# Gated cross-attention and mixture of experts on one core: ten instead of twelve row-maximum tiles ahead of the attention, the turn of the maxima one step later, and rows of ones spread by transfers

## The chip, the core and the metric

The kernel runs on one core of one Trainium2 chip. A core has five engines that run their own instruction lists side by side: PE (TensorE, matrix products, with PEld for its weight loads), DVE (VectorE), ACT (ScalarE), POOL (GpSimd) and SP (SyncE, which here only issues DMA transfers). They wait for each other through semaphores. The metric is the device time of one launch in microseconds. The kernel before took 764.62 us in the median of 3 runs (763.82 to 765.73).

## What is computed

The reference, cut to what matters (4 batches, 512 queries, 1024 keys, width 256, 16 heads of width 16, 8 routed experts of which each token takes 2, and one shared expert):

```python
q, k, v = heads(layernorm(x) @ Wq.T + bq), heads(ctx @ Wk.T + bk), heads(ctx @ Wv.T + bv)
attn = softmax(q @ k.T / 4) @ v
x = x + tanh(g_xattn) * (join_heads(attn) @ Wo.T + bo)
h = layernorm(x)
cw = top2(softmax(h @ gate_w + gate_b))
x = x + tanh(g_ffn) * (swiglu_expert(h, shared) + sum_e cw[e] * swiglu_expert(h, e))
```

The biases and weights are scaled so that products of plain bfloat16 numbers would be too coarse. So queries and keys are split into three bfloat16 parts each, and six products of parts are stacked as 96 rows of the contraction.

## The kernel before

**Phase A** (PE lines up to L1396) makes queries, keys and values, batch by batch. For each batch PE multiplies three 512-wide blocks: two of the context (keys and values) and one of the normalised x (queries). ACT copies and adds the bias (`biased`, L744 and L745, and the value copies L753), DVE makes the second parts (L1002, L1003), the rounding remainders (L979) and the layer norm (`variances`, L951 to L957, and `normalise`, L962 to L968), POOL makes the third parts (L575). SP stores all of it to DRAM and loads it back in the stacked layout as `qst` and `kst`. `kst` holds the keys of four slots; slot u is heads 4u to 4u+3. Rows 96 to 98 of `kst` are ones; the same rows of `qst` are filled with the three bfloat16 parts of the negated row maximum of the scores. A score matmul contracts all 99 rows, so the maximum is subtracted inside the product.

At its very start POOL sets those three rows of ones for all slots with one memset (L554), after two memsets on `vst`. DVE then works out the layer norm of the first batch, ACT takes a square root in it (L716), and PE turns the normalised rows (`turn`, L1324) between its first and its second block.

**The attention** is 16 units (4 batches by 4 slots), each of 8 steps (one per 128 keys). What PE does in step k of a unit is written out by hand: the scores of heads 0 and 1 for the step two ahead (`LEAD = 2`, L1423), the products with the values for this step (L1450), the scores of heads 2 and 3 for two steps ahead, and then two maximum tiles (`max_tile`, L1405). A maximum tile is the 128 by 1024 score block of one head and 128 queries; DVE reduces it to 128 negated maxima (L1058). ACT takes the exponentials of the scores (L795).

Each unit needs 16 such tiles. They run ahead: `FIRST` = 12 of the next unit's are made before the attention begins, for unit 1. Then the steps of unit n make the 4 that are missing for unit n+1 (steps 0 and 1) and 12 for unit n+2 (steps 2 to 7). When unit n+1 has its 16, its maxima go this way:

1. PE turns them with a 128 by 16 transpose at the end of step `MAX_TURN` = 2 (`turn_max`, L1334).
2. ACT copies the result in step `MAX_COPY` = 3, behind the exponentials of its first head (`copy_max`, L772).
3. POOL splits it into three bfloat16 parts with four small instructions (`split_max`, L561 to L567).
4. SP sends each part into a row of `qst` (`load_max`, three transfers, L400).
5. PE waits for the three transfers (`m_ld`) before the first score of unit n+1. That score is made two steps ahead, so it stands at the start of step 6 of unit n. All that PE has after it in its list waits too.

Between phase A and the loop PE runs the `FIRST` maximum tiles and, from the sixth on, one of the first 8 scores beside each (`BEFORE = 5`). In unit 0 POOL has one more instruction ahead of its first split in the loop: it multiplies the output bias by the gate (L614), and waits for that bias, which SP loads at L454 behind the loads of slots 2 and 3.

**The end of the attention.** In the last units no later unit is left to make maxima for. Unit 14 makes only the missing ones for unit 15. After those the router and output projection begin beside the attention, from step 3 of unit 14 (`ROUTER_AT`, stages 0 to 12): PE turns stored attention outputs (`r_attn`, L1511) and multiplies them with the output weights (L1518). Stage 0 waits until all maxima are reduced, since it writes where they were. From `TAIL` on, the scores of heads 2 and 3 also go into room of the maxima. On SP, the transfers of unit 15's maxima are queued behind two loads (L473) that wait for the router's turns of stages 0 and 2.

**After it** come the shared expert, the routing table, and 39 tiles of 128 routed tokens through their experts (L1656 to L1694), added to the output by POOL.

Of the kernel before, what the change touches and what calls it, by code (L numbers as in the profile page):

```python
# [29 lines left out]
BF16 = mybir.dt.bfloat16  # L30
# [6 lines left out]
P = 128  # L37
# [3 lines left out]
QT = NQ // P  # L41
KT = NK // P
HG = 4
NG = NH // HG
UNITS = NB * NG
TERMS = ((0, 0), (0, 1), (1, 0), (1, 1), (0, 2), (2, 0))
SROWS = len(TERMS) * DH
MROWS = SROWS + 3
# [17 lines left out]
BLK = 512  # L66
# [4 lines left out]
def build(nc, x, ctx_in, gates, wqkv, bqkv, wo, bo, gate_w, gate_b, wexp, b1, b2, ident, tri, out):  # L71
# [11 lines left out]
    with ExitStack() as es:  # L83
        sb = lambda name, shape, dt=F32, st=es: st.enter_context(nc.sbuf_tensor(name, shape, dt))
        ps = lambda name, shape, st=es: st.enter_context(nc.psum_tensor(name, shape, F32))
        sem = lambda name: es.enter_context(nc.semaphore(name))
# [9 lines left out]
        W0 = nc.sbuf_base  # L96
# [4 lines left out]
        b1_p = sb("b1_p", [NE * 4, 3, P], BF16, sP)  # L101
        sP.close()
        sb("early_weights", [P, EARLY, WU, UNIT], F32R)
        trimask = sb("trimask", [P, NR, NR])
        tg_in = sb("tg_in", [P, 2])
        tg = sb("tg", [P, 2])
# [65 lines left out]
        kst = sb("kst", [MROWS, NG, HG, NK], BF16, sB)  # L172
# [53 lines left out]
        v_full = sem("v_full"); v_taken = sem("v_taken")  # L226
        qk_st = [sem(f"parts_stored{c}") for c in range(3)]
        v_st = [sem(f"v_stored{s}") for s in range(4)]
        pads = sem("pads"); ones_k = sem("ones_k"); cw_ones = sem("cw_ones")
        unit_ld = [sem(f"unit_in{s}") for s in range(NG)]  # L230
        m_ld = [sem(f"max_in{s}") for s in range(NG)]
        m_full = sem("m_full"); m_free = sem("m_free")
# [60 lines left out]


        TILES = HG * QT
        FIRST = 12
        REST = TILES - FIRST
        AHEAD = TILES + FIRST
        MAX_TURN = 2
        MAX_COPY = 3  # L300
        LEAD = 2


# [8 lines left out]

        TAIL = KT * (UNITS - 2) + 2 + LEAD
        ROUTER_AT = KT * (NG - 2) + 3

        def score_bank(s, j):
# [10 lines left out]
        def max_tiles(u, step):  # L329

            for j in (2 * step, 2 * step + 1):
                yield (j, 1, FIRST + j) if j < REST else (j, 2, j - REST)

        def exists(last, u):
            return not last or u < NG
# [5 lines left out]
        def _(sp):  # L341
# [41 lines left out]
            def load_unit(b, u):  # L383

                for t, (qp, kp) in enumerate(TERMS):
                    rows = slice(t * DH, (t + 1) * DH)
                    heads = slice(u * HG * DH, (u + 1) * HG * DH)
                    sp.dma_start(qst[rows, u], q_parts[b, qp, heads, :].rearrange("(h d) t -> d h t", d=DH)
                                 ).then_inc(unit_ld[u], 16)
                    sp.dma_start(kst[rows, u], k_parts[b, kp, heads, :].rearrange("(h d) t -> d h t", d=DH)  # L390
                                 ).then_inc(unit_ld[u], 16)
# [10 lines left out]
            def first_unit():  # L402

                for c in range(3):
                    sp.wait_ge(qk_st[c], 32 + 32)
                load_unit(0, 0)

            stores(0, True)
            stores(1, True, first_unit)
# [125 lines left out]
        def _(pool):  # L535
# [15 lines left out]
            nc.gpsimd.memset(vst[:, :, :, :, DH:DH + 1].rearrange("p a b h v -> p (a b h) v"), 1.0).then_inc(pads, 1)  # L551
            pool.wait_ge(pads, 1)

            nc.gpsimd.memset(kst[SROWS:MROWS], 1.0).then_inc(ones_k, 1)  # L554
            pool.wait_ge(ones_k, 1)


            def split_max(n, parity):
# [153 lines left out]
        def _(act):  # L712
# [88 lines left out]
            def unit_exps(b, u, last):  # L801
                n = 4 * b + u
                for k in range(KT):
                    ahead = exists(last, u + (k + LEAD) // KT)
                    for j in range(HG):
                        if ahead:
                            exponentials(8 * n + k + LEAD, (k + LEAD) % 4, j)
                        if k == MAX_COPY and j == 0 and exists(last, u + 1):

# [126 lines left out]
        def _(dve):  # L936
# [123 lines left out]

            for i in range(FIRST):
                reduce_tile(TILES + i, 1, i)
# [250 lines left out]
        def _(pe):  # L1313
# [112 lines left out]

            pe.wait_ge(f_taken, 2 + 6 * NB)
            pe.wait_ge(v_taken, 2 + 4 * NB)
            pe.wait_ge(ones_k, 1)
            pe.wait_ge(unit_ld[1], 16 * 12)  # L1430
            BEFORE = 5
            for i in range(FIRST):
                max_tile(TILES + i, 1, i)
                if i == BEFORE:
                    pe.wait_ge(m_ld[0], 48)
                if i >= BEFORE:
                    score_tile((i - BEFORE) // HG, 0, (i - BEFORE) // HG, (i - BEFORE) % HG)
            for i in range(FIRST - BEFORE, LEAD * HG):
                score_tile(i // HG, 0, i // HG, i % HG)
# [14 lines left out]
            def unit(b, u, last):  # L1454
                n = 4 * b + u
                for k in range(KT):
# [17 lines left out]
                    for j, off, i in tiles:  # L1474
# [3 lines left out]
                        max_tile(AHEAD + TILES * n + j, (u + off) % NG, i)  # L1478
                    if k == MAX_TURN and exists(last, u + 1):
                        turn_max(n + 1, (u + 1) % 2, AHEAD + TILES * n + REST)  # L1480
# [289 lines left out]
```

## Time and profile before

| | |
|---|---|
| span of the profiled execution | 764.7 us |
| median of 3 runs (lowest, highest) | 764.62 us (763.82, 765.73) |
| PE busy | 672.2 us, 88% |
| DVE busy | 498.5 us, 65% |
| ACT busy | 425.6 us, 56% |
| POOL busy | 238.4 us, 31% |
| 240 maxima reductions on DVE, L1058 | 282.6 us, 1220 ns each |
| 488 score matmuls into psS, L1423 | 154.3 us, 389 ns each |
| 1024 value matmuls, L1450 | 138.5 us, 613 ns each |
| 480 maximum matmuls, L1405 | 128.0 us, 387 ns each |
| mean granted TensorE clock | 0.948 of full |

Busy time says how long an engine had an instruction running; matmuls overlap, so a busy PE counts each stretch once. The span is one execution by the profiler. The share of PE over the whole is a mean over stages: phase A up to 121 us, the attention up to about 541 us, the shared expert and routing up to about 607 us, and the routed tiles. What a change is worth is read in its own stage.

### The profile page before, as it was taken

Reading aid. Unit: us, or ns where it says so; the run is one execution under the profiler, and the core shown is the slowest. Engines: PE = TensorE matmul, PEld = TensorE weight load, DVE = VectorE, ACT = ScalarE, POOL = GpSimd, SP = SyncE. Lnnn points to the kernel's source line nnn. Section 1 sums busy time; section 2 is a strip of 40 time slices with the busy share of each in tenths; the row PEclk is TensorE's granted clock in tenths of the full one; section 3 lists DMA queues with packets and bytes.
Section 4 is the critical chain, followed back from the end, with each engine's and each line's share of the span. In section 5 each row is a group of like instructions: output and inputs, shape, how many; then the busy total and the mean of one; then the engine's idle time right before and its main releaser. Section 6 shows DMA issues by size and latency. Waiting matters only on the chain.

```text
span 764.7 us, 12596 instructions
## 1 busy us (share of the span) xinstructions
PE 672.2 (88%) x3616; PEld 337.7 (44%) x3616; DVE 498.5 (65%) x791; ACT 425.6 (56%) x842; POOL 238.4 (31%) x236
## 2 busy tenths in 40 slices
PE   3787659699999999999999999788669899999980
PEld 3675532133333333333333333433547677777750
DVE  5899888578888888888888886375267433232320
ACT  3665345467777777777777777455122234343430
POOL 8433232312434224430002221001744024444441
PEclk9999898899999999999999999899979999999995
DMA  8799769665677976787634500100795524545334
GB/s 268 275 241 361 138 228 167 101 97 104 177 163 145 212 185 188 163 164 140 92 57 69 101 1 2 55 0 9 269 427 189 155 51 86 86 80 86 59 45 125
DMA packets 80954, 106.36 MB, mean 139 GB/s; under 512 B 15616, under 2 KB 62890, under 8 KB 79949
## 3 DMA queue, kind: packets, MB, share of 16 engines
q1 hardware_dynamic: 70400, 78.04, 43.6%
q0 software_dynamic: 10512, 27.79, 14.0%
q8 instruction: 22, 0.36, 0.2%
q14 instruction: 20, 0.16, 0.1%
HBM read 62.10 MB, written 45.60 MB: 141 GB/s over the span
## 4 chain that ended last, share of the span: by engine, by line
PE 71%; issue 13%; DVE 5%; POOL 4%; DMA 3%; another core or an unknown queue 2%; SPq 1%; ACT 0%; POOLq 0%; DVEq 0%; ACTq 0%
PE psO L1450 16%; PE psS L1423 15%; PE psM L1405 12%; PE psH L1668 8%; PE psY L1694 4%; POOL parts L575 3%; PE psH L1624 2%; PE psH L1665 2%; PE psX L1518 1%; PE psH L1679 1%; PE psX L1656 1%; PE psY L1691 1%; PE psO L1493 1%; DMA acc<-ysb,zg 1%
## 5 line engine op out<-in xcount | busy, mean ns | idle before, releaser
L795 ACT ACTIVATE pr<-psS 128x512 f32<-128x512 f32 x488 | 266.6, 595 | 108.8 <-PE psS L1423 108.7
L1058 DVE TENSOR_REDUCE mneg<-psM 128x1 f32<-128x1024 f32 x240 | 282.6, 1220 | 68.1 <-PE psM L1405 68.0
L1423 PE MATMUL psS<-qst,kst 99*128 99x512 bf16 x488 | 154.3, 389 | 11.2 <-DMA qst<-msb 10.7
L1450 PE MATMUL psO<-pr,vt 128*32 128x512 f32 x1024 | 138.5, 613 | 0.0
L1405 PE MATMUL psM<-kst,qst 96*128 96x512 bf16 x480 | 128.0, 387 | 6.4 <-DVE mneg L1058 4.1
L1423 PEld LDWEIGHTS psS<-qst,kst 99*128 99x128 bf16 x488 | 40.0, 97 | 160.0 <-ACT pr L795 130.0
L705 POOL DMA_INDIRECT acc<-ysb,zg x39 | 60.2, 1542 | 100.6 <-DMA acc<-ysb,zg 54.7
L1294 DVE TENSOR_TENSOR rg<-psH,rs 128x256 f32<-128x256 f32 x39 | 16.6, 425 | 90.3 <-ACT rs L906 83.2
L1405 PEld LDWEIGHTS psM<-kst,qst 96*128 96x128 bf16 x480 | 46.3, 98 | 65.6 <-DVE mneg L1058 10.6
L561 POOL TENSOR_TENSOR msb<-mcp,none 16x128 bf16<-16x128 f32 x16 | 6.2, 389 | 209.8 <-ACT mcp L772 209.7
L1668 PE MATMUL psH<-wall,zgT 128*128 x234 | 65.0, 413 | 0.0
L669 POOL DMA_INDIRECT zs<-zx,slot_u x32 | 32.3, 1010 | 78.4 <-DVE slot_u L1175 69.5
L575 POOL TENSOR_TENSOR parts<-kf,parts 128x512 bf16<-128x512 f32 x24 | 30.9, 1290 | 59.3 <-DVE parts L1003 59.2
L1668 PEld LDWEIGHTS psH<-wall,zgT 128*128 128x128 f32 x234 | 40.9, 188 | 15.8 <-issue 8.8
L906 ACT ACTIVATE rs<-psH 128x256 f32<-128x256 f32 x39 | 14.9, 383 | 54.0 <-PE psH L1668 54.0
L1694 PE MATMUL psY<-wall,gT 128*128 x234 | 37.6, 296 | 0.0
L1450 PEld LDWEIGHTS psO<-pr,vt 128*32 128x32 f32 x1024 | 20.3, 108 | 36.4 <-issue 35.1
L1624 PE MATMUL psH<-zT,wall 128*128 128x512 f32 x96 | 28.9, 455 | 7.3 <-DVE g L1242 4.0
L918 ACT ACTIVATE ysb<-psY,zg 128x256 f32<-128x256 f32 x39 | 18.5, 474 | 28.2 <-PE psY L1694 26.1
L1363 PE MATMUL psV<-wAH,tH 128*128 128x256 f32 x64 | 17.8, 367 | 16.8 <-DVE tL L979 16.8
L1694 PEld LDWEIGHTS psY<-wall,gT 128*128 128x128 f32 x234 | 29.9, 188 | 4.7
L744 ACT ACTIVATE kf<-psF,bq_s 128x512 f32<-128x512 f32 x24 | 16.5, 689 | 20.4 <-PE psF L1377 16.4
(240 smaller groups left out, 855.2 us busy)
## 6 DMA issues: line engine op xcount, KB each, us to landing
kst<-k_parts SPq DMA_DIRECT2D x96, 128.0 KB, 5.8
w_parts<-wraw POOLq DMA_DIRECT2D x14, 768.0 KB, 4.7
wall<-w_parts SPq DMA_DIRECT2D x7, 1536.0 KB
v_pad<-vst SPq DMA_DIRECT2D x16, 512.0 KB, 7.7
vt<-v_pad SPq DMA_DIRECT2D x16, 512.0 KB, 7.6
wraw<-wexp POOLq DMA_DIRECT2D x9, 768.0 KB, 6.3
k_parts<-parts SPq DMA_DIRECT2D x16, 384.0 KB, 5.8
qst<-q_parts SPq DMA_DIRECT2D x96, 64.0 KB, 5.6
```

Of the source, the lines that this page charges most:

```text
L575: nc.gpsimd.tensor_tensor(parts[:, c, m, 2], kf[:, m], parts[:, c, m, 1], ALU.subtract).then_inc(k_ok, 1)
L669: nc.gpsimd.indirect_dma_start(out=zs[:, :], out_offset=bass.IndirectOffsetOnAxis(ap=slot_u[:, b, k * QT + t:k * QT + t + 1], axis=0), in_ ...
L705: nc.gpsimd.indirect_dma_start(out=acc[:, :], out_offset=bass.IndirectOffsetOnAxis(ap=zg[:, i % ZG, 264:265].bitcast(U32), axis=0), in_=ys ...
L795: nc.scalar.activation(pr[:, slot, j], score_bank(s, j), ACT.Exp, scale=SCALE).then_inc(e_done, 1)
L918: nc.scalar.activation(ysb[:, i % YB], psQ[:, i % 2, 0:D], ACT.Identity, scale=zg[:, i % ZG, bass.ds(e + D, 1)]).then_inc(ry_ok, 1)
L1058: V.tensor_reduce(mneg[:, parity, i:i + 1], psM[:, i % 2], X_AXIS, ALU.max, negate=True).then_inc(m_free, 1)
L1405: last = mm(psM[:, i % 2, half * BLK:(half + 1) * BLK], qst[0:SROWS, slot, h, qt * P:(qt + 1) * P], kst[0:SROWS, slot, h, half * BLK:(half ...
L1423: mm(score_bank(s, j), kst[:, slot, j, kt * P:(kt + 1) * P], qst[:, slot, j], start=True, stop=True).then_inc(s_full, 1)
L1450: last = mm(psO[j * VW:(j + 1) * VW, u % 2], vt[:, u, k, j * VW:(j + 1) * VW], pr[:, k % 4, j], start=(k == 0), stop=(k == KT - 1), skip_g ...
L1624: last = mm(psH[:, j, ab], w1(SH, wp)[:, 4 * k + m], zT(b)[:, zp, k], start=(i == 0 and k == 0), stop=(i == 2 and k == DT - 1))
L1668: last = mm(psR[:, i % 2], zgT[:, i % 2, zp, k], wall[:, bass.ds(w + (12 * wp + 4 * k), 4)].rearrange("p a c -> p (a c)"), start=False, st ...
L1694: last = mm(psQ[:, i % 2, 0:D], gT[:, i % 2, gp, k], wall[:, bass.ds(w + (12 * wp + 8 + 2 * k), 2)].rearrange("p a c -> p (a c)"), start=F ...
```

## The change

Three things are changed.

- `FIRST` goes from 12 to 10. Ten maximum tiles of unit 1 are made before the attention, six missing ones in steps 0 to 2 of each unit, and ten for the unit after in steps 3 to 7. Unit 14 makes six.
- `MAX_TURN` goes from 2 to 3 and `MAX_COPY` from 3 to 4, and `TAIL` by one, since the maxima are complete one step later. `LEAD`, and so the place of the wait for the transfers, stays.
- The memset of 3 by 16384 ones on `kst` becomes a memset of 3 by 2048 ones on a `strip`, and eight transfers on SP copy the strip into the slots, two per slot, behind the loads of x and ahead of the loads of the second batch's context.

```diff
+        strip = nc.alloc_sbuf_tensor_at("strip", [MROWS - SROWS, HG, QT * P], BF16, offset=W0 + 8192)
...
-        FIRST = 12
+        FIRST = 10
...
-        MAX_TURN = 2
-        MAX_COPY = 3
+        MAX_TURN = 3
+        MAX_COPY = 4
...
-        TAIL = KT * (UNITS - 2) + 2 + LEAD
+        TAIL = KT * (UNITS - 2) + 3 + LEAD
...
+            sp.wait_ge(strip_ok, 1)
+            for u in range(NG):
+                for half in range(2):
+                    sp.dma_start(kst[SROWS:MROWS, u, :, half * BLK:(half + 1) * BLK], strip[:]).then_inc(ones_k, 16)
+
             stores(0, True)
...
-            nc.gpsimd.memset(kst[SROWS:MROWS], 1.0).then_inc(ones_k, 1)
-            pool.wait_ge(ones_k, 1)
+            nc.gpsimd.memset(strip[:], 1.0).then_inc(strip_ok, 1)
...
-            pe.wait_ge(ones_k, 1)
+            pe.wait_ge(ones_k, 16 * 2 * NG)
```

Lines of the changed kernel are 5 or 6 further down in ACT, DVE, POOL and PE (L1405 is L1410, L1334 is L1339, L772 is L777).

ACT, units 12 and 13 (the first two of the last batch), before. `pr<-psS` is an exponential, `mcp` the copy of the turned maxima, `osb` the copy of a unit's output in its last step:

```order
378 L795 ACTIVATE pr<-psS 128x512 x13
379 L772 COPY mcp<-psO 16x128
380 L795 ACTIVATE pr<-psS 128x512 x17
381 L815 COPY osb<-psO 128x512
382 L795 ACTIVATE pr<-psS 128x512 x15
383 L772 COPY mcp<-psO 16x128
384 L795 ACTIVATE pr<-psS 128x512 x17
385 L815 COPY osb<-psO 128x512
```

and now:

```order
378 L800 ACTIVATE pr<-psS 128x512 x17
379 L777 COPY mcp<-psO 16x128
380 L800 ACTIVATE pr<-psS 128x512 x13
381 L820 COPY osb<-psO 128x512
382 L800 ACTIVATE pr<-psS 128x512 x19
383 L777 COPY mcp<-psO 16x128
384 L800 ACTIVATE pr<-psS 128x512 x13
385 L820 COPY osb<-psO 128x512
```

The copy has moved back by four exponentials, which is one step. The last exponential ahead of a unit's end has kept its place.

PE, unit 14, steps 2 to 4, before. `psM<-kst,qst` are maximum tiles, `psS` and `psM<-qst,kst` scores, `psO<-pr,vt` the values, `psO<-idn,mneg` the turn of the maxima, `psX<-idn,a_in` the router's first turn:

```order
692 L1423 MATMUL psS<-qst,kst 128x512 x2
693 L1450 MATMUL psO<-pr,vt 32x512 x4
694 L1423 MATMUL psM<-qst,kst 128x512 x2
695 L1334 MATMUL psO<-idn,mneg 16x128
696 L1423 MATMUL psS<-qst,kst 128x512 x2
697 L1450 MATMUL psO<-pr,vt 32x512 x4
698 L1423 MATMUL psM<-qst,kst 128x512 x2
699 L1511 MATMUL psX<-idn,a_in 128x128 x8
700 L1423 MATMUL psS<-qst,kst 128x512 x2
```

and now, from the two extra tiles of step 2 on:

```order
690 L1428 MATMUL psS<-qst,kst 128x512 x2
691 L1410 MATMUL psM<-kst,qst 128x512 x4
692 L1428 MATMUL psS<-qst,kst 128x512 x2
693 L1455 MATMUL psO<-pr,vt 32x512 x4
694 L1428 MATMUL psM<-qst,kst 128x512 x2
695 L1339 MATMUL psO<-idn,mneg 16x128
696 L1516 MATMUL psX<-idn,a_in 128x128 x8
697 L1428 MATMUL psS<-qst,kst 128x512 x2
```

Step 2 has four more matmuls, and the turn of the maxima now stands directly ahead of the router's first turn, in step 3.

SP, between the input loads and the first stores, now (before, the same list without the row of eight):

```order
14 L358 DMA xs<-x 128x4x256 x3
15 L412 DMA kst<-strip 3x4x512 x8
16 L366 DMA ctxt<-ctx 128x2x512 x2
17 L375 DMA v_pad<-vst 128x2x512 x2
18 L381 DMA k_parts<-parts 128x3x512 x2
```

The context loads of the second batch and the first stores stand behind the eight.

## Rows read from the trace of the kernel before

**Rows 1.** PE's waits in the attention loop, 151 to 470 us (engine line <- releaser: us, times, longest)
```profile
PE psS L1423 <- DMA qst<-msb: 6.6, 1, 6.6
```

**Rows 2.** Busy time by stage: PE, PEld, DVE, ACT, POOL (instructions), clock, DMA share, GB/s
```profile
170.00:470.00 300.00, 300.00 (x1697) 95.39 (x1697) 247.88 (x231) 229.39 (x433) 77.82 (x91) 1.00 0.61 126
```

**Rows 3.** Timeline of unit 2, turn to first score of unit 3 (start, us, engine, line)
```profile
191.63 0.27 PE L1334 MATMUL psO<-idn,mneg 128*16 128x128 f32 x1
...
194.86 1.80 SPq L400 DMA_DIRECT2D qst<-msb  x3
...
195.16 1.06 PE L1450 MATMUL psO<-pr,vt 128*32 128x512 f32 x8
...
198.04 1.07 PE L1450 MATMUL psO<-pr,vt 128*32 128x512 f32 x8
...
200.35 0.65 PE L1423 MATMUL psS<-qst,kst 99*128 99x512 bf16 x2
```

**Rows 4.** Instructions on `msb`, 150 to 470 us (count, ns min/median/max, first and last start)
```profile
L400 SPq DMA_DIRECT2D qst<-msb x39: 502/582/592, 171.4 to 454.9; - x39
...
DMA to landing us min/median/max: 1.7/1.8/2.9
```

**Rows 5.** The chain that ended last, start of unit 1's scores (start, us, what)
```profile
148.99 1.77 DMA qst<-msb
150.88 1.03 PE psS L1423 x2
```

**Rows 6.** Timeline of unit 0, up to its wait in step 6
```profile
133.71 1.37 SPq L454 DMA_DIRECT2D cmp<-bo  x1
...
145.23 0.61 POOL L614 TENSOR_TENSOR cmp<-cmp,tg 128x256 f32<-128x256 f32 x1 [23.88 <-DMA cmp<-bo]
...
147.79 1.78 SPq L400 DMA_DIRECT2D qst<-msb  x3
```

**Rows 7.** Timeline between phase A and unit 0
```profile
113.08 14.13 DVE L1058 TENSOR_REDUCE mneg<-psM 128x1 f32<-128x1024 f32 x12
...
127.33 1.06 PE L1450 MATMUL psO<-pr,vt 128*32 128x512 f32 x8
```

**Rows 8.** Timeline of the first 30 us
```profile
4.47 13.75 POOL L554 MEMSET kst<- 3x16384 bf16 x1
...
11.57 1.57 SPq L365 DMA_DIRECT2D ctxt<-ctx  x2
...
15.12 3.12 DVE L957 TENSOR_SCALAR veps<-mv 128x4 f32<-128x4 f32 x1
...
20.97 1.09 PE L1324 MATMUL psT<-idn,zA 128*128 128x128 f32 x8 [1.37 <-DVE zA L968]
...
26.16 0.17 DVE L957 TENSOR_SCALAR veps<-mv 128x4 f32<-128x4 f32 x1
...
26.48 0.69 ACT L744 ACTIVATE kf<-psF,bq_s 128x512 f32<-128x512 f32 x1 [0.93 <-PE psF L1377]
...
29.00 1.14 ACT L733 CAST tH<-ctxt 128x512 fp32r<-128x512 f32 x2
```

**Rows 9.** DMA issues of the whole run (KB each, median us to landing)
```profile
ctxt<-ctx SPq DMA_DIRECT2D x8, 512.0 KB, 6.7
```

**Rows 10.** Timeline of unit 14, steps 2 to 6
```profile
470.87 2.36 DVE L1058 TENSOR_REDUCE mneg<-psM 128x1 f32<-128x1024 f32 x2 [0.53 <-PE psM L1405]
...
473.28 0.60 PE L1423 MATMUL psM<-qst,kst 99*128 99x512 bf16 x2 [0.54 <-DVE mneg L1058]
...
473.72 0.27 PE L1334 MATMUL psO<-idn,mneg 128*16 128x128 f32 x1
...
475.80 1.04 PE L1511 MATMUL psX<-idn,a_in 128*128 128x128 f32 x8
...
485.51 2.38 SPq L400 DMA_DIRECT2D qst<-msb  x3
...
489.17 1.04 PE L1423 MATMUL psS<-qst,kst 99*128 99x512 bf16 x2 [4.07 <-DMA qst<-msb]
```

More of the change, by code:

```diff
@@ L228, in build @@
         v_st = [sem(f"v_stored{s}") for s in range(4)]
-        pads = sem("pads"); ones_k = sem("ones_k"); cw_ones = sem("cw_ones")
+        pads = sem("pads"); ones_k = sem("ones_k"); strip_ok = sem("strip_ones"); cw_ones = sem("cw_ones")
         unit_ld = [sem(f"unit_in{s}") for s in range(NG)]
```

## The prediction

> **What bounds the kernel now.** I read the shares by stage first, then PE's waits inside the attention, then the timeline of one unit, and last the two places that the change touches outside the loop. In the attention loop from 170 to 470 us PE is busy for all of the 300 us at full clock, DVE for 248 and ACT for 229 [rows 2]. So in this stage the reader is to see that PE sets the pace, and that DVE has about a sixth of its time to spare. From 151 to 470 us PE waits for something else just once: 6.6 us for the transfers of unit 1's maxima [rows 1]. Any new wait of PE in the loop, and any work added to it, is paid in full; work that only moves within it costs nothing.
>
> A step takes 198.04 - 195.16 = 2.88 us [rows 3]. The time that matters for the change is the way of a unit's maxima. In unit 2, PE starts their turn at 191.63, SP starts the first of the three transfers at 194.86 (3.23 us later, through ACT and POOL), and PE's first score that needs them starts at 200.35, that is 8.72 us after the turn [rows 3]. SP needs 0.58 us for each issue and a transfer lands a median 1.8 us after its issue began (1.7 to 2.9) [rows 4]. So the last of three lands 3.23 + 2 x 0.58 + 1.8 = 6.19 us after the turn. After such a landing PE starts its score about 0.12 us later: 148.99 + 1.77 = 150.76, and the score is at 150.88 [rows 5]. The way takes 6.31 us, and 8.72 are there: 2.41 us of slack, less than the 2.88 of a step.
>
> **The change part by part.**
>
> *The turn a step later, units 2 to 14.* The six missing tiles are complete after step 2, so the turn stands at the end of step 3 and ACT's copy a step later too, as the two lists of ACT show: four exponentials, one step. The first score of the next unit stays in step 6. ACT, POOL and SP do the same work in the same order behind the turn, so the way stays 6.31 us, while the time for it shrinks to 8.72 - 2.88 = 5.84 us. PE waits 0.47 us in each unit. Queued behind this score in PE's list are the rest of step 6 and everything after; PE has no slack in which to win it back [rows 2]. The wait comes at the ends of units 1 to 13, which is 13 times: 39 transfers in three each [rows 4]. 13 x 0.47 = 6.1 us. With a landing of 2.2, between the median and the longest, it would be 0.87 each, 11.3 us; with 1.7 it would be 0.37 and 4.8 us. Since the waits can only add where a landing is late (2.9 is the longest), the mean lies above the median, and I take 0.55 each, 7.1 us, with 4.8 and 11.3 as bounds.
>
> The Trainium skill ("DMA: Bandwidth & Descriptors", section "Anatomy of one DMA — SWDGE (gpsimd) path") gives every transfer a fixed cost of about 2.0 us that does not shrink with its size. The rows of these small transfers say 1.8. By the page the wait would be 0.67 each, and an estimate for 13 of them 8.7 us. It speaks against the change in the same direction as the rows; I go by the rows.
>
> *Two tiles fewer ahead of the loop.* The reductions run without a gap there, 14.13 us for 12, and PE begins step 0 at 127.33, behind them [rows 7]. Two fewer are 2 x 14.13 / 12 = 2.4 us, of which some is kept by the 8 scores that have to be made in any case; about 2.1 us are won. But the next stop is not PE's: in unit 0 POOL's split of unit 1's maxima stands behind L614, which waits until 145.23 for the bias, issued by SP at 133.71; the transfers go out at 147.79 [rows 6]. That chain hangs on the end of phase A and on the DMA queues, not on the tiles. PE comes 2.1 us earlier to its wait of 6.6 us [rows 1] and waits 8.7. The gain here is 0. The later turn in unit 0 is hidden in this wait as well, being more than 5 us ahead of 145.23. If the bias came earlier too, the gain would be up to 2.4.
>
> *The two tiles at the end.* They are made in step 2 of unit 14, which had none. Before, the last reductions ended at 473.23, the scores that take the maxima's room came at 473.28, the turn 0.44 us later, and the router's first turn at 475.80 [rows 10]. Now the last reductions end a step later, at 476.1, the scores come at 476.16, the turn at 476.6 and the router's turn right behind it, at 476.7. So the router is 0.9 us late. The maxima of unit 15 go out only at 485.51, behind SP's wait for the router's turns, and PE waits 4.07 us for them [rows 10]. Their split is still done by then, so this stop only moves with the router: +0.9 us, no second price. Bounds: 0.4 (if PE makes good its wait for DVE) to 1.5.
>
> *The memset and the transfers.* The memset runs from 4.47 for 13.75 us, to 18.22 [rows 8]. DVE's small L957 at 15.12 takes 3.12 us and ends at 18.24; the same instruction takes 0.17 at 26.16 [rows 8]. So it was held until the memset ended. The Trainium skill ("SBUF — State Buffer", section "SBUF: two separate sides") says that a GpSimd operation and some DVE operations lock a shared port pair for a whole instruction; by that rule, as by the rows, a memset of an eighth of the length (1.7 us, over by 6.2) leaves L957 free. The normalised rows come about 2.9 us earlier, but PE was idle for only 1.37 us ahead of its turn at 20.97; before that it was busy with its first block. ACT's next work waits for PE (0.93 us at 26.48) [rows 8], so phase A moves forward by PE's 1.37 us. I take -1.4. Bounds: -2.9 (if ACT and POOL use all of it), and +1.0 for the other side: the eight issues take SP 8 x 0.58 = 4.6 us [rows 4], so the context loads of the second batch go out near 16 instead of 11.57 [rows 8]. They land 6.7 us later [rows 9], near 23, and ACT needs them at 29.00 - 1.4 [rows 8]. That hides them, with some 4 us to spare.
>
> **Sum**, against the profiled span of 764.7 us, which is practically the median of the runs: -1.4 + 0 + 7.1 + 0.9 = +6.6, 771.3 us.
>
> **The rivals.**
>
> *The transfers land in time.* The turn or ACT's copy might come quicker than in the timeline of before, or the landing, a step later and with the loads of the next batch done, might be under the median. It needs the way to shrink from 6.31 to 5.84 us. For it: landings of 1.7 exist [rows 4]. Against it: even 1.7 leaves 0.37, and the 3.23 us of ACT, POOL and SP are a chain of fixed work. Then 764.7 - 1.4 + 0.9 = 764.2; with the largest gain at the start and ahead of the loop 759.9. This is the one on the other side. It decides from a landing of 1.33 us.
>
> *Each wait costs more.* Landings near the longest, or a restart of PE that costs ACT's exponentials a gap as well, would make it 1.1 us in each unit: 14.3 in place of 7.1, 778.5 us. For it: 2.9 us is in the rows, with loads in the queues [rows 4]. Against it: the median is near the minimum.
>
> *The start gives nothing.* The strip's transfers delay the first context loads or stores so much that phase A stays where it was: 764.7 + 7.1 + 0.9 = 772.7 us. For it: SP issues in order. Against it: the 4 us computed above.
>
> *The start gives it all* (-2.9): 769.8 us.
>
> **How the numbers follow.** The forecast, with the start at about -1.4, has 0.55; the start giving nothing 0.12 and giving all 0.10, both with the same wait; the costlier waits 0.10; the transfers in time, or nearly so, 0.13. The range of 8 in 10 is 767.0 (the smaller wait of 4.8, the start at -2.9, the end at 0.4) to 778.0 (wait of 11.3, the start at 0, the end at 1.5 and a little of the third case). No change means within 0.3%, 762.3 to 766.9 us, about what a measurement of this kernel can tell. The last case falls into it for the most part: same 0.09, faster 0.04. Slower 0.87.
>
> **What would show it.** In the profile after, PE's waits in the loop should list the scores' line with the maxima's transfers as releaser about 13 times at 0.3 to 0.9 us, besides one near 8.7 us in unit 0 and one near 4 in unit 14. Steps without it should still take 2.88 us. The memset should be near 1.7 us, L957 (now L962) under 0.3 us both times, and PE's turn in the first batch without an idle stretch ahead of it. DVE's row of ten reductions should be near 11.8 us. I would be wrong if PE shows no such waits in units 1 to 13, if unit 1's transfers go out more than 2 us earlier than the shift of phase A explains, or if the context cast of the second batch waits for its load.

## The result, and the profile after

The changed kernel takes 772.38 us (median of 12 runs, 770.77 to 774.15), the kernel before 765.23 us (12 runs). The ratio is 1.0071 (95% interval 1.0047 to 1.0095), so the change costs about 5.4 us by the ratio (3.6 to 7.3); the two medians alone differ by 7.2 us, which is at the edge of that. In the table of experiments below, too, the ratio is the recorded one and not that of the two medians. The forecast was 771.3 us, slower. In the profiled executions the span goes from 764.7 to 769.4 us.

I read the profile after in the order of the prediction. First PE's waits between 115 and 500 us (engine line <- releaser: us, times, longest):

```profile
PE psS L1428 <- DMA qst<-msb: 17.5, 15, 9.5
PE psM L1428 <- DVE mneg L1063: 0.5, 1, 0.5
```

Fifteen waits for the maxima's transfers stand where the same stretch of before had two ([rows 1] shows the one of unit 0, [rows 10] the one of unit 14). One of them is in unit 0 (9.5 us), one in unit 14 (3.9), and 13 are new. The view by stage says the same; it answers to [rows 2]: PE is idle for 4.0 of 300 us at full clock, where it was never idle.

```profile
170.00:470.00 300.00, 295.97 (x1666) 93.42 (x1663) 243.13 (x225) 224.93 (x427) 78.15 (x92) 1.00 0.64 126
```

The timeline of unit 2 shows how one of the 13 comes about. It answers to [rows 3]:

```profile
195.65 0.27 PE L1339 MATMUL psO<-idn,mneg 128*16 128x128 f32 x1
...
196.68 0.24 ACT L777 COPY mcp<-psO 16x128 f32<-16x128 f32 x1
...
197.00 0.39 POOL L566 TENSOR_TENSOR msb<-mcp,none 16x128 bf16<-16x128 f32 x1 [16.30 <-ACT mcp L777]
...
198.88 1.81 SPq L401 DMA_DIRECT2D qst<-msb  x3
...
199.18 1.06 PE L1455 MATMUL psO<-pr,vt 128*32 128x512 f32 x8
...
201.97 0.60 PE L1428 MATMUL psS<-qst,kst 99*128 99x512 bf16 x2 [0.33 <-DMA qst<-msb]
...
202.50 1.06 PE L1455 MATMUL psO<-pr,vt 128*32 128x512 f32 x8
```

From the turn to SP's first transfer it is 198.88 - 195.65 = 3.23 us, as before. From the turn to the score it is 6.32 us, where the prediction had worked out 6.31. The step with the wait takes 202.50 - 199.18 = 3.32 us in place of 2.88, so a wait costs 0.44 us, though the row shows 0.33. Where the other 0.11 us go the rows do not say. The turns of the units are now 23.97 us apart (171.61 for unit 1, 459.20 for unit 13), before 23.52. The transfers themselves were a little quicker than the median of before:

```profile
DMA to landing us min/median/max: 1.6/1.7/2.1
```

At the start the memset and the instruction of DVE that it had held read so (answering to [rows 8]):

```profile
4.47 1.79 POOL L560 MEMSET strip<- 3x2048 bf16 x1
...
10.00 6.18 SPq L412 DMA_DIRECT2D kst<-strip  x8
...
14.04 0.17 DVE L962 TENSOR_SCALAR veps<-mv 128x4 f32<-128x4 f32 x1
...
18.82 1.03 PE L1329 MATMUL psT<-idn,zA 128*128 128x128 f32 x8
...
24.28 0.69 ACT L749 ACTIVATE kf<-psF,bq_s 128x512 f32<-128x512 f32 x1 [0.93 <-PE psF L1382]
```

L962 has gone from 3.12 to 0.17 us, and PE's turn has no idle stretch ahead of it. ACT's L749 comes at 24.28 instead of 26.48. Some 2.2 us are won here. This execution's first weight load also landed earlier (ACT's first work on it is at 6.95 in place of 8.03), but that isn't what won them: in e6 below that work starts only at 8.37, and the same instruction of ACT still comes at 24.44. The context cast of the second batch, which the prediction named as a sign of being wrong, starts at 26.79 without a wait. By the end of phase A only 0.56 us of the gain is left. DVE's row of reductions ahead of the attention, against 113.08 in [rows 7]:

```profile
112.52 12.02 DVE L1063 TENSOR_REDUCE mneg<-psM 128x1 f32<-128x1024 f32 x10
```

Unit 0 (answering to [rows 6]; the last row is PE's wait, 6.6 us in [rows 1]):

```profile
146.51 0.61 POOL L619 TENSOR_TENSOR cmp<-cmp,tg 128x256 f32<-128x256 f32 x1 [25.72 <-DMA cmp<-bo]
...
149.07 1.78 SPq L401 DMA_DIRECT2D qst<-msb  x3
...
152.14 1.03 PE L1428 MATMUL psS<-qst,kst 99*128 99x512 bf16 x2 [9.53 <-DMA qst<-msb]
```

The bias landed 1.3 us later than before, though SP issued it 0.5 us earlier (133.23 against 133.71), and all that hangs on it moved with it.

The account of the span: unit 1's first score, behind the wait of unit 0, is at 152.14 against 150.88 (+1.26). From there to unit 15's first score it is 344.04 against 338.29 us (+5.75). The rest is 273.2 against 275.5 (-2.3). That sums to +4.7.

The +5.75 are less than thirteen waits and the two tiles together (5.7 and 0.9), because a part of the stretch has another clock. Behind the wait of unit 0 PE works for some microseconds at a granted clock of 0.50, that is at 1.2 GHz and not 2.4 (busy time and clock of 150 to 155 us, before and then now):

```profile
150.00:155.00 5.00, 4.12 (x14) 0.87 (x15) 0.00 (x0) 1.73 (x4) 2.68 (x1) 0.50 0.02 4
```

```profile
150.00:155.00 5.00, 2.86 (x11) 0.45 (x12) 0.00 (x0) 1.09 (x2) 3.87 (x2) 0.50 0.03 6
```

From unit 1's first score to PE's turn of unit 0's output, where that stretch lies, it is 8.19 us before and 7.55 now, 0.64 less. From there to unit 15's first score it is 336.49 against 330.10 us, 6.4 more, and that is what the waits and the tiles add up to.

### The profile page after: what moved, and what is told of

The parts are those of the page before. It is cut to its first block, busy times and chain, and to the rows that moved or that the text cites. A ratio compares the mean times of both kernels' runs of the same rounds, so it can differ in the third digit from the quotient of the medians.

```text
span 769.4 us, 12603 instructions
## 1 busy us (share of the span) xinstructions
PE 673.8 (88%) x3616; PEld 337.6 (44%) x3616; DVE 496.4 (65%) x791; ACT 426.2 (55%) x842; POOL 226.9 (29%) x236
## 4 chain that ended last, share of the span: by engine, by line
PE 61%; issue 17%; POOL 7%; DMA 5%; DVE 3%; SPq 2%; ACT 2%; another core or an unknown queue 1%; POOLq 0%; ACTq 0%; DVEq 0%
PE psO L1455 12%; PE psS L1428 12%; PE psM L1410 9%; PE psH L1673 8%; PE psY L1699 4%; POOL parts L580 3%; DMA qst<-msb 3%; PE psH L1629 2%; SPq L401 2%; PE psH L1670 2%; PE psX L1523 1%; PE psH L1684 1%; PE psX L1661 1%; PE psY L1696 1%; DMA acc<-ysb,zg 1%
## 5 line engine op out<-in xcount | busy, mean ns | idle before, releaser
L1410 PE MATMUL psM<-kst,qst 96*128 96x512 bf16 x480 | 127.4, 386 | 5.7 <-DVE mneg L1063 3.4
L1410 PEld LDWEIGHTS psM<-kst,qst 96*128 96x128 bf16 x480 | 46.4, 98 | 64.0 <-DVE mneg L1063 8.9
L1629 PE MATMUL psH<-zT,wall 128*128 128x512 f32 x96 | 26.9, 433 | 4.0 <-issue 4.0
L749 ACT ACTIVATE kf<-psF,bq_s 128x512 f32<-128x512 f32 x24 | 16.5, 688 | 23.8 <-PE psF L1382 18.0
```

The lines of the kernel that those rows point to most:

```text
L1410: last = mm(psM[:, i % 2, half * BLK:(half + 1) * BLK], qst[0:SROWS, slot, h, qt * P:(qt + 1) * P], kst[0:SROWS, slot, h, half * BLK:(half ...
L1629: last = mm(psH[:, j, ab], w1(SH, wp)[:, 4 * k + m], zT(b)[:, zp, k], start=(i == 0 and k == 0), stop=(i == 2 and k == DT - 1))
```

## The experiments

Every kernel below states bounds on the counts that POOL loads and waits for in the routed part; e0 shows what that costs. Ratios are to the kernel before, run beside each on the same chip, and only ratios are compared from one group to another. e9 and later ran where the kernel before takes 754 to 755 us in place of 765 to 769. Their turns are 23.5 us apart all the same; what is shorter lies behind the attention (from the end of unit 14 it is 252.3 us in e9 and 265.7 in e7), and the cause stays open.

| kernel | median us | before, beside it | ratio (95%) |
|---|---|---|---|
| e0 before, bounds stated | 766.92 | 767.46 | 1.0001 (0.9978 to 1.0024) |
| e1 after, long memset back | 775.00 | 767.46 | 1.0081 (1.0054 to 1.0107) |
| e2 before + strip | 765.01 | 767.46 | 0.9973 (0.9952 to 0.9993) |
| e3 before + turn a step later | 775.07 | 767.46 | 1.0083 (1.0051 to 1.0114) |
| e4 after + parts sent when ready | 766.11 | 769.11 | 0.9962 (0.9934 to 0.9990) |
| e6 after + bias later | 769.88 | 769.11 | 1.0000 (0.9976 to 1.0024) |
| e7 after + both | 762.88 | 769.11 | 0.9902 (0.9864 to 0.9939) |
| e8 before + both | 762.66 | 769.11 | 0.9907 (0.9874 to 0.9940) |
| e9 e7 + last unit earlier | 743.08 | 754.89 | 0.9851 (0.9824 to 0.9879) |
| e11 e9 + loads later | 737.41 | 754.89 | 0.9768 (0.9739 to 0.9797) |
| e12 e11's four edits on before | 739.32 | 754.89 | 0.9790 (0.9762 to 0.9817) |
| e13 e12 + strip | 737.69 | 753.80 | 0.9799 (0.9762 to 0.9836) |

### Which part of the change costs

*e0_before_bounded*: the kernel before with the bounds stated.

> The kernel before, with bounds asserted on the four counts that POOL reads from its table ahead of each group of routed additions (the other runs have this too, so they are read against this one). Both theories: the same time as the kernel before within 0.3%; the asserts lie on POOL in the routed tiles, which PE bounds. In the attention no difference: turns of the maxima 23.52 us apart.

Measured: ratio 1.0001. The other load costs nothing that can be measured.

*e1_memset_back*: the changed kernel with the memset of all slots, and no strip.

```diff
...
-            nc.gpsimd.memset(strip[:], 1.0).then_inc(strip_ok, 1)
+            nc.gpsimd.memset(kst[SROWS:MROWS], 1.0).then_inc(ones_k, 1)
...
```

> The changed kernel with the long memset on kst in place of the strip and its eight transfers. Theory W (the price is a wait of PE for the maxima's transfers, 0.45 us in each of units 1 to 13, which comes from the turn a step later): the 13 waits of 0.3 to 0.4 us stay, turns 23.97 us apart, and the whole is 5.5 to 8.5 us over the kernel before: the strip's gain of 0.5 to 1.5 us is missing. Theory S (the strip's transfers, through the DMA queues and SP, cost the time): it comes back to within 2 us of the kernel before.

*e2_strip_alone*: the kernel before with the strip and its eight transfers, nothing else.

```diff
...
-            nc.gpsimd.memset(kst[SROWS:MROWS], 1.0).then_inc(ones_k, 1)
+            nc.gpsimd.memset(strip[:], 1.0).then_inc(strip_ok, 1)
...
```

> The kernel before with only the strip and its eight transfers; twelve tiles ahead and the turn in step 2 stay. Theory W: -0.3 to -1.5 us; DVE's small instruction no longer waits for the memset, the first 80 us come about 2 us earlier, and most of it is lost again by the end of phase A; turns 23.52 us apart and one wait for the maxima, in unit 0, of 6.6 to 8.5 us. Theory S: +4 us or more.

*e3_turn_alone*: the kernel before with twelve tiles and the long memset, but the turn and the copy a step later.

```diff
-        MAX_TURN = 2
-        MAX_COPY = 3
+        MAX_TURN = 3
+        MAX_COPY = 4
```

> The kernel before with only the turn in step 3 and the copy in step 4: same tiles, same memset. Theory W: all of the price is here: 13 waits of 0.3 to 0.4 us, turns 23.97 us apart, +5.9 us (+4.8 to +7), unit 0 and unit 14 unchanged. A rival, theory T (the price lies in where the tiles are made, since DVE and PE meet otherwise): 0 us here and turns 23.52 us apart.

Measured: e3, with nothing but two numbers changed, costs all that the change costs and a little more (1.0083). e1, the change without its strip, costs 1.0081 where the whole change costs 1.0071, a difference within the intervals. e2 is the one part that gains (0.9973, about 2.1 us, a little more than I had expected). PE's waits from 115 to 500 us in e3, and one of the 13 in its timeline:

```profile
PE psS L1424 <- DMA qst<-msb: 16.0, 15, 8.3
```

```profile
196.41 0.28 PE L1335 MATMUL psO<-idn,mneg 128*16 128x128 f32 x1
...
199.63 1.80 SPq L400 DMA_DIRECT2D qst<-msb  x3
...
202.71 0.60 PE L1424 MATMUL psS<-qst,kst 99*128 99x512 bf16 x2 [0.31 <-DMA qst<-msb]
```

The way from the turn to the score is 6.30 us, as in the changed kernel (6.32). In e2 the same view of the waits has no such row but the two of before:

```profile
PE psS L1429 <- DMA qst<-msb: 11.5, 2, 7.1
```

From unit 1's first score to unit 15's e3 takes 343.33 us where e0 takes 337.58. That is 5.75 us more, as good as 13 times 0.44 (5.7), in a kernel with all twelve tiles. So the price is the turn's, and neither the tiles' nor the strip's.

### Taking the 13 waits away

*e4_parts_when_ready*: the changed kernel, in which SP sends each of the three parts when POOL has made it, and not all three when the last is made.

```diff
                 for s in range(3):
+                    if s < 2:
+                        sp.wait_ge(m_chain, 3 * m + 1 + 2 * s)
+                    else:
+                        sp.wait_ge(mt_split, m + 1)
                     sp.dma_start(qst[SROWS + s:SROWS + s + 1, u], msb[:, u % 2, s, :]).then_inc(m_ld[u], 16)
```

> The changed kernel, but SP sends each of the three parts of the maxima as soon as POOL has made it, instead of all three behind the last. The first two issues of 0.58 us then lie beside POOL's work, so the way from the turn to the landing is about 1.2 us shorter: 5.1 us where 5.84 are there. Theory W: the 13 waits of units 1 to 13 are gone, turns 23.52 us apart, unit 0's wait 1.2 us shorter; 6 to 8 us faster than the changed kernel, that is 0 to 2 us faster than the kernel before. Rival: if PE's waits were a side show and something else slows the steps, the turns stay 23.97 us apart and it gains 1 us.

Measured: 0.9962, the 13 waits are gone, and the turns are 23.52 us apart again. Waits and unit 2's timeline in e4:

```profile
PE psS L1431 <- DMA qst<-msb: 11.2, 2, 7.4
```

```profile
191.22 0.27 PE L1342 MATMUL psO<-idn,mneg 128*16 128x128 f32 x1
...
192.57 0.39 POOL L568 TENSOR_TENSOR msb<-mcp,none 16x128 bf16<-16x128 f32 x1 [15.79 <-ACT mcp L780]
192.99 2.10 SPq L405 DMA_DIRECT2D qst<-msb  x3
```

The first transfer goes out 1.77 us after the turn in place of 3.23, and the last issue ends at 195.09, that is 3.87 us after the turn in place of 5.04 (198.88 + 1.81 - 195.65). The 1.17 us that this saves are more than the 0.47 that were missing. The ratio falls from 1.0071 to 0.9962, about 8 us, more than the 13 waits are worth (13 x 0.44 = 5.7); from unit 1's first score to unit 15's it is 339.63 us in place of 344.04, a gain of 4.4 (the work at half clock behind unit 0's wait took 1.1 us more here: 8.65 against 7.55 to the turn of unit 0's output), and the attention begins about 3 us earlier than in the changed kernel (first reduction at 109.61), which is scatter of phase A (below).

### Taking unit 0's wait away

*e6_bias_later*: the changed kernel, in which POOL multiplies the bias by the gate behind its first split in the loop, not ahead of it. *e7_both* has this and the edit of e4. *e8_before_both* is the kernel before with both.

```diff
-            pool.wait_ge(bo_in, 16)
...
-            nc.gpsimd.tensor_tensor(bo_s, bo_s, tg[:, 0:1].to_broadcast([P, D]), ALU.mult).then_inc(u_ok, 1)
...
                 split_max(n + 1, (n + 1) % 2)
+                if n == 0:
+                    pool.wait_ge(bo_in, 16)
...
+                    nc.gpsimd.tensor_tensor(bo_s, bo_s, tg[:, 0:1].to_broadcast([P, D]), ALU.mult).then_inc(u_ok, 1)
```

> The changed kernel, but POOL waits for the output bias and scales it behind the first split of the loop instead of ahead of it. If the two tiles' gain of 2 us is lost in unit 0's wait (9.5 us) for a split that stands behind the bias, that wait shrinks to 0.3 to 0.5 us like the other thirteen, and the stretch of half clock behind it goes too: 9 to 11 us faster than the changed kernel. Rival: the DMA queues, not POOL's order, hold the transfers of unit 1's maxima; then they land late all the same and it gains 0 to 3 us.

> The changed kernel with both: each part sent when ready, and the bias behind the first split. No wait for the maxima in units 0 to 13, turns 23.52 us apart from the first: 15 to 18 us faster than the changed kernel, 754 to 757 us.

> The kernel before (twelve tiles, turn in step 2, long memset) with the same two edits. No wait in unit 0: 8 to 10 us faster than the kernel before. Read against the changed kernel with both edits it shows what ten tiles and the strip are worth when no wait hides them: by my terms 2.1 us (tiles ahead) less 0.8 us (tiles in unit 14) and 1.3 us (strip), so this one should be about 2.6 us slower than that one. Rival: the turn a step later still costs, and they are equal.

Measured: e6 1.0000, so by the ratios about 5.4 us less than the changed kernel: not the 9 to 11 of the theory, and more than the 0 to 3 of the rival. e7 is about 13 us faster than the changed kernel, not 15 to 18, and e8 about 7 us faster than the kernel before, not 8 to 10. In all three a wait in unit 0 is left. The split did come early. Timeline of e6 in unit 0:

```profile
136.77 0.39 POOL L566 TENSOR_TENSOR msb<-mcp,none 16x128 bf16<-16x128 f32 x1 [17.40 <-ACT mcp L780]
...
138.64 1.78 SPq L401 DMA_DIRECT2D qst<-msb  x3
...
144.38 0.61 POOL L659 TENSOR_TENSOR cmp<-cmp,tg 128x256 f32<-128x256 f32 x1 [5.76 <-DMA cmp<-bo]
...
146.12 1.03 PE L1431 MATMUL psS<-qst,kst 99*128 99x512 bf16 x2 [4.76 <-DMA qst<-msb]
```

The transfers are issued by 140.42, and PE can start only at 146.12. The chain that ended last names it in one row (start, us, what):

```profile
139.84 6.15 DMA qst<-msb
```

A transfer of 4 KB takes 6.15 us here and 1.7 in the loop. What stands ahead of it is seen in e7 by the DMA issues of 125 to 150 us (x count, KB each, median us to landing) and the 16 DMA engines' busy tenths in 40 slices of that stretch:

```profile
DMA  9999999999999999999999999999940000000000
...
kst<-k_parts SPq DMA_DIRECT2D x4, 128.0 KB, 12.2
vt<-v_pad SPq DMA_DIRECT2D x1, 512.0 KB, 13.1
wo_s<-wo SPq DMA_DIRECT2D x1, 256.0 KB, 13.1
...
qst<-msb SPq DMA_DIRECT2D x3, 4.0 KB, 6.0
```

The engines are full until 144 us with the loads of units 1 to 3 and of the output weights, and the small transfers land about 2 us after that stops. e7 and e8 are equal (0.9902 and 0.9907), where I had expected e8 to be slower by the two tiles: PE reaches its first step 4.6 us later in e8 (128.9 against 124.3), and both then wait for the end of their loads (4.6 us in e7, 2.0 in e8). Behind its longer wait e7 also works longer at half clock (below), so at the turn of unit 0's output e7 is only 0.8 us ahead (154.11 against 154.93), and it loses that again by unit 15.

### Last unit and loads

*e9_last_unit_earlier*: e7, and SP sends unit 15's maxima between the two loads of stored attention, not behind both.

```diff
             for u in range(NG):
-                unit_dmas(NB - 1, u, True)
+                if u != 2:
+                    unit_dmas(NB - 1, u, True)
...
                         sp.dma_start(a_in[:], attn[b]).then_inc(a_ld, 16)
+                        if b == 1:
+                            unit_dmas(NB - 1, 2, True)
```

> The changed kernel with each part sent when ready, the bias behind the first split, and in addition the transfers of unit 15's maxima put between the two loads of the stored attention on SP, not behind both. Theory: the wait of 4.1 us of PE at unit 15's first score (all kernels so far have 3.8 to 4.4 there) comes only from SP's order, since the split is done long before: it goes to under 1 us, and the time is 3 to 4 us under that of the kernel with both (762.9), 759 to 760. Rival: the first load still stands ahead of them, and its wait for the stores or the load itself keeps the wait at 2 us or more: 761 to 763.

*e11_loads_later*: e9, and the loads of unit 3 and of the output weights go out behind the transfers of unit 1's maxima. By their sizes these are 1.9 MB (6 x 64, 6 x 128, 512 and 256 KB), not the 1.4 of the expectation. *e12_before_loads_later* has the same four edits on the kernel before, *e13_twelve_strip* has them and the strip, with twelve tiles and the turn after step 2.

```diff
             load_values(0, 2)
+            for s in range(3):
+                sp.dma_start(b1_parts[s].rearrange("(q p) -> q p", p=P), b1_p[:, s]).then_inc(bp_st, 16)
+                sp.dma_start(b2_parts[s].rearrange("(e d) -> e d", d=D), b2_p[:, s]).then_inc(bp_st, 16)
+            sp.dma_start(bo_s, bo).then_inc(bo_in, 16)
+            load_max(0, 1, 1)
             load_unit(0, 3)
```

> The kernel before this one in the list, and in addition the loads of unit 3 and of the output weights (1.4 MB) issued behind the transfers of unit 1's maxima and not ahead of them. Theory: unit 1's maxima wait 6 us for older loads in the queues; with those gone they land within about 2.5 us of their issue, PE's wait of 4.6 us at unit 1's first score goes to under 1 us, and the time is about 4 us less than without: 755 to 757. Rival: the loads of units 1 and 2 and the values, which still stand ahead, keep the queues full as long, and the wait stays above 3 us: 759 to 760.

> The same four edits on the kernel before (twelve tiles ahead, the turn after step 2, the long memset). Theory: once no transfer holds unit 0, the two tiles fewer and the free start of the changed kernel count: this one is 2 to 4 us slower than the changed kernel with the same edits, 758 to 760, with PE's first step about 2 to 3 us later and no more wait at unit 1's first score. Rival: the two are equal within 1 us, as they were with the queues full, since the start is lost again in phase A and the two tiles are only made later.

> The kernel before with the four edits of the last two kernels (parts sent when ready, bias later, unit 15 earlier, unit 3's loads later) and with the strip, but with twelve tiles ahead and the turn after step 2: of the change only the strip. Theory: the ten tiles are worth little even with the queues freed, since what is not made ahead is made in unit 14 (0.7 to 0.8 us) and the later turn has 2.9 us less of slack for its transfers: this kernel is equal to the one with all of the change within 1 us (ratio to before 0.975 to 0.979), and PE's first score of unit 2 has no wait. Rival: the ten tiles give their 2 us in full: this kernel is at 0.979 to 0.981, as the one without the strip.

Measured: e9 is 0.9851 after e7's 0.9902, 0.5% or about 4 us. The two intervals overlap, but the trace is plain: the wait for unit 15's maxima is gone from its list, only unit 0's is left, and from the turn of the maxima in unit 14 to the turn of that unit's output it is 17.51 us in place of 23.38. e11 takes unit 0's wait too (0.9768, another 5.7 us by the medians beside each other, 4.5 by the spans). Waits of e9, then of e11:

```profile
PE psS L1436 <- DMA qst<-msb: 3.8, 1, 3.8
```

```profile
PE psS L1438 <- DMA qst<-msb: 1.2, 1, 1.2
```

In e11 the DMA issues of 125 to 150 us now have the small transfers at the landing of the loop, with the engines idle from 132 us until the loads that were put off begin:

```profile
DMA  9999999999910000000000000001589999999999
...
qst<-msb SPq DMA_DIRECT2D x3, 4.0 KB, 1.7
```

The wait of 1.2 us that is left is a new one, at unit 2's first score: the loads that were put off now stand ahead of unit 2's transfers.

```profile
167.82 0.60 PE L1438 MATMUL psS<-qst,kst 99*128 99x512 bf16 x2 [1.17 <-DMA qst<-msb]
```

The three kernels without unit 0's wait can be compared by one instruction, PE's turn of a unit's output: at the end of unit 0 and of unit 14. First e11, then e12, then e13:

```profile
148.74 0.60 PE L1508 MATMUL psO<-idn,osb 128*128 128x128 f32 x4
...
485.21 0.60 PE L1508 MATMUL psO<-idn,osb 128*128 128x128 f32 x4
```

```profile
151.58 0.60 PE L1503 MATMUL psO<-idn,osb 128*128 128x128 f32 x4
...
485.67 0.60 PE L1503 MATMUL psO<-idn,osb 128*128 128x128 f32 x4
```

```profile
148.04 0.60 PE L1508 MATMUL psO<-idn,osb 128*128 128x128 f32 x4
...
482.18 0.60 PE L1508 MATMUL psO<-idn,osb 128*128 128x128 f32 x4
```

The stretch is 336.47 us with the change (e11), 334.09 and 334.14 with twelve tiles and the early turn (e12, e13). The difference of 2.35 us is 1.3 of the wait at unit 2 (the turns on both sides of it are 24.81 us apart, not 23.52), 0.2 in a later unit where the turns are 23.72 apart, and 0.9 that is left for the two tiles in unit 14. Ahead of the loop the two tiles give DVE's 14.26 - 11.99 = 2.3 us back. So the ten tiles are worth nothing in e11.

e12 was expected 2 to 4 us slower than e11. It is 1.9 slower by the medians and 1.1 by the spans, and the intervals overlap. For e13 I had expected a ratio of 0.975 to 0.979, the rival 0.979 to 0.981. The measured 0.9799 lies in the rival's range, but its interval (0.9762 to 0.9836) holds both. The trace speaks against the rival: e13 is 3.0 us ahead of e11 at that late turn, and its span is 1.8 us shorter. Whether it is the better kernel stays open at this precision. Both beat the kernel before by 2.0 to 2.3%, the changed kernel by about 3%.

The same instruction shows something for which the prediction has no term, though the expectation of e6 names it: the wait in unit 0 costs more than its length. With no wait the way from PE's first step to the turn of unit 0's output is 22.56 us, with ten tiles and with twelve. With a wait, its length does not make up the difference:

| kernel | first step | turn of unit 0's output | between them | wait | left over |
|---|---|---|---|---|---|
| before | 127.33 | 159.07 | 31.74 | 6.60 | 2.6 |
| after | 125.66 | 159.69 | 34.03 | 9.53 | 1.9 |
| e7 | 124.28 | 154.11 | 29.83 | 4.63 | 2.6 |
| e8 | 128.85 | 154.93 | 26.08 | 1.99 | 1.5 |
| e9 | 122.91 | 153.91 | 31.00 | 3.83 | 4.6 |
| e11 | 126.18 | 148.74 | 22.56 | none | 0 |

What is left over is the clock. In e9 PE had worked at a granted clock of 1.00 up to 140 us, was idle for 3.83, and then was busy for all of 144 to 153 us at 0.50, the lower of its two levels; in e11 it stays at 1.00. First e9, then e11:

```profile
144.00:153.00 9.00, 9.00 (x29) 1.87 (x28) 2.36 (x2) 4.21 (x8) 3.51 (x2) 0.50 0.01 2
```

```profile
126.00:160.00 34.00, 33.94 (x193) 10.48 (x193) 26.51 (x24) 25.48 (x49) 7.10 (x7) 1.00 0.77 117
```

So e11 wins 8.4 us in unit 0 for a wait of 3.8. It does not show in full at the end of unit 14, where e11 is 3.7 us ahead (485.21 against 488.95), since e11 entered the loop 3.3 us later in that execution and has its own wait in unit 2. Why the stretch at 0.50 is 9 us long in e9 and 3 in e8 the runs don't show. The wait of unit 15's maxima had such a tail too: the 5.9 us that e9 wins there are 4.1 of the wait and 1.8 more.

## Why the prediction was right, and where a term was off

**The turn a step later: right in mechanism, a quarter too large.** Predicted were 13 waits of 0.55 us, 7.1 in all. The trace has 13 waits, in the predicted places, with the predicted releaser. Nearly each costs 0.44 us, the turns being 23.97 against 23.52 us apart: 5.7. (The last two are shorter, 0.15 and 0.24 us of idle time in place of 0.33.) The way was right to 0.01 us (6.32 against 6.31). I had put a mark-up of 0.08 on 0.47 for late landings, on the ground that the longest was 2.9 us [rows 4]; sent a step later they landed quicker, 1.7 (1.6 to 2.1), as they land more slowly where they are sent earlier: 2.4 in e8, 2.5 in e12 and 2.6 in e13, the longest 4.1 to 4.3. Why they do was not looked at further. The section of the Trainium skill that the prediction drew on, "Anatomy of one DMA — SWDGE (gpsimd) path" in "DMA: Bandwidth & Descriptors", gives its 2.0 us for transfers that GpSimd issues. These are issued by SP, and the rows, which the sum went by, were nearer: 1.8, then 1.7. e3 gives the whole slowdown with this edit alone, and e4 takes the waits away by shortening the way by more than was missing: both halves of the argument, cause and slack, are shown. The rival in which the transfers land in time fell: it needed 1.33 us. So did the costlier waits. (Its largest gain of 759.9 us was added up wrongly: 764.2 - 1.5 - 2.4 is 760.3.)

**Two tiles fewer ahead of the loop: gain 0 predicted, none found.** PE reached its first step 1.7 us earlier (125.7 against 127.33 in [rows 7]), and its wait in unit 0 grew from 6.6 to 9.5 us. The score behind it came 1.3 us later, not at the same time, because the bias landed at 146.51 instead of 145.23 in that execution. The prediction named the bias as what holds the split; e6 shows that behind it stands a second stop, the DMA engines' work on the loads, some 4 us under the first. My sentence "If the bias came earlier too, the gain would be up to 2.4" was wrong as it stood: e7 and e8, with the bias out of the way, are equal. The half clock behind the wait stood in no term either; here it differed by 0.64 us between before and after, in the change's favour. Only with the loads put off as well does the earlier start reach unit 1 (e11), and then unit 14 and unit 2 take it back.

**The two tiles at the end: right.** Predicted +0.9. From e11 against e13 it is 0.9 when the wait at unit 2 and the 0.2 us are taken off; e9, with no wait in between, has 335.04 us for the same stretch as e13's 334.14, which is 0.9 again.

**The start: the mechanism right, the size uncertain.** Memset, L962 and PE's turn did what was said. I had limited the gain to PE's own idle 1.37 us. Over all kernels, the first reduction ahead of the attention starts at 111.2 us on average in the eight with the strip (109.6 to 112.9) and at 113.75 in the six without it (112.8 to 114.7). That is 2.6 us, near the bound of 2.9 that I had set as "ACT and POOL use all of it". By the whole time the strip is worth less or is not resolved: 2.1 us in e2, 0.8 between e1 and the changed kernel, and e13 against e12 has a higher ratio but a lower time (0.9799 against 0.9790, 737.69 against 739.32 us). In the one pair that the prediction was compared with, only 0.56 of it arrived; over 90 to 115 us the granted clock was 0.87 there and 0.94 before. But e13 has 0.84 and starts at 111.11, so the clock alone doesn't explain the scatter, and what does stays open.

**The sum.** +6.6 predicted, +5.4 by the ratio, +4.7 in the profiled pair. The waits were 1.4 us too dear. The start was 1.2 us too small a gain by the mean of the reductions, 0.8 too large a one in this pair. The rest (-2.3 us after unit 15's score in that pair) lies within the scatter of that part: 273.2 to 278.1 us over before, after and e0 to e3. So the direction and the 13 waits were reasoned out, while it is in part luck that the sum came within 1.2 us: the scatter of the parts that the change does not touch is larger than that.

## What to carry to other kernels

Work out the slack of a handover from the timeline, from the first instruction of its way to the one that needs it, before moving the start by a step: two numbers in a table cost 0.8% here because the way had 2.41 us of slack and the step is 2.88. Where a unit's result leaves in several parts, send each when it is made: here that shortened the way by 1.17 us and took away all 13 waits. Count behind a wait of PE also what it does to the clock: a wait of 3.8 us cost 8.4 in e9. And where a wait ends at a chain's last link, look at what stands behind that link before counting its gain: the bias hid the DMA engines' load queue, and the queue hid most of what the two tiles give.

## What the runs showed of the hardware

- Three transfers of 4 KB from SBUF to SBUF landed a median 1.7 us after their issue in the loop of the changed kernel (1.8 before, up to 2.6 in e13), and 6.0 us in e7 when the 16 DMA engines were full with loads issued before them, on the same queue. With 1.9 MB of those loads put behind them they landed in 1.7 us (e11).
- SP takes 0.77 us for each of the eight issues from the strip (6.18 / 8), against 0.6 for a one-row part of the maxima. I had counted 0.58. It cost nothing here.
- A memset of POOL held DVE's 128 by 4 instruction until it ended, in every kernel with the long memset: 3.12, 2.94, 4.36, 2.72, 3.98 and 3.87 us, ending each time at 18.24 or 18.25, and 0.17 us in all eight with the short one.
- After PE had been idle for 2.0 to 9.5 us in unit 0, its granted clock was 0.50 (1.2 GHz) for the next 3 to 9 us of its work, and 1.00 (2.4 GHz) again after that; this cost 1.5 to 4.6 us on top of the wait. Neither the length of the wait nor anything else that was looked at orders these.
